# Cross-attention in a decoder layer: the mask's fetch one unit ahead, the row maxima on other steps

## The reference

```python
q = jnp.einsum('oc,bct->bot', Wq, target) + bq[None, :, None]
k = jnp.einsum('oc,bcs->bos', Wk, source) + bk[None, :, None]
v = jnp.einsum('oc,bcs->bos', Wv, source) + bv[None, :, None]
# q, k, v reshaped to (b, 16 heads, 16, 512)
dot = jnp.einsum('bhdt,bhds->bhts', q, k) / math.sqrt(HEAD_DIM)
mask = target_mask[:, :, :, None] * source_mask[:, :, None, :]
dot = mask * dot - (1.0 - mask) * NEG
amap = jax.nn.softmax(dot, axis=-1) * mask
out = jnp.einsum('bhts,bhds->bhdt', amap, v)
```

## Time and profile before

| | |
|---|---|
| median of 3 runs (lowest, highest) | 4616.4 us (4610.94, 4616.81) |
| the profiled execution's own time | 4613.8 us |
| its span, first to last instruction | 4612.0 us |
| mean granted TensorE clock | 0.959 |
| TensorE, VectorE, ScalarE busy | 91%, 70%, 48% of the span |

### The profile page before, as it was taken

One profiled execution on the slowest core, in us unless ns is written; L12 is line 12 of the kernel. 1 busy time (PEld: TensorE's weight loads), 2 busy tenths in 40 slices (PEclk: granted clock), 3 DMA queues, 4 the chain that ended last, 5 costly groups with the idle time before them and its releaser, 6 DMA issues. The chain is left out here.

```text
span 4612.0 us, 78540 instructions
## 1 busy us (share of the span) xinstructions
PE 4198.6 (91%) x27808; PEld 3133.2 (68%) x27808; DVE 3208.1 (70%) x6426; ACT 2230.6 (48%) x4057; POOL 623.2 (14%) x571
## 2 busy tenths in 40 slices
PE   3999999999999999999999999995788888489998
PEld 2777777777777777777777777773344444168887
DVE  3788888888888888888888888884555555532222
ACT  2555655555555655555555555552344444311111
POOL 1010010000110001100011000102133323411110
PEclk8999999999999999999999999996889989789999
DMA  2000000000000000000000000002545453000001
GB/s 70 1 15 15 11 15 11 16 10 11 15 15 11 10 11 15 15 11 11 11 16 15 11 13 9 15 1 51 82 81 86 81 85 64 38 23 19 19 14 37
DMA packets 66482, 122.17 MB, mean 26 GB/s; under 512 B 10476, under 2 KB 12396, under 8 KB 65548
## 3 DMA queue, kind: packets, MB, share of 16 engines
q1 hardware_dynamic: 63628, 115.69, 11.7%
q10 hardware_dynamic: 2432, 1.05, 0.1%
HBM read 93.05 MB, written 21.50 MB: 25 GB/s over the span
## 5 line engine op out<-in xcount | busy, mean ns | idle before, releaser
L387 PE MATMUL pj<-xh,w_hi 128*128 128x512 f32 x1536 | 688.2, 448 | 31.4 <-ACT conv_k L618 17.0
L387 PE MATMUL pj<-xh,w_lo 128*128 128x512 f32 x1536 | 607.7, 396 | 0.0
L387 PE MATMUL pj<-xl,w_hi 128*128 128x512 f32 x1536 | 602.7, 392 | 0.0
L1503 DVE TENSOR_REDUCE row_max<-s 128x1 f32<-128x512 f32 x512 | 341.8, 685 | 261.0 <-PE s L1257 256.9
L1437 ACT ACTIVATE probs<-s 128x512 f32<-128x512 f32 x512 | 290.3, 595 | 332.7 <-PE s L1281 265.8
L998 POOL CAST w_hi<-w_raw 128x512 fp32r<-128x512 f32 x96 | 73.8, 769 | 2083.8 <-PE pj L387 2079.7
L387 PEld LDWEIGHTS pj<-xh,w_hi 128*128 128x128 f32 x1536 | 291.1, 189 | 80.7 <-issue 32.3
L387 PEld LDWEIGHTS pj<-xh,w_lo 128*128 128x128 f32 x1536 | 289.2, 188 | 67.2
L689 ACT ACTIVATE kk_masked<-tp 128x512 f16<-128x512 f32 x320 | 191.4, 598 | 291.2 <-PE tp L493 288.1
L387 PEld LDWEIGHTS pj<-xl,w_hi 128*128 128x128 f32 x1536 | 292.7, 191 | 49.9 <-issue 14.8
L1281 PE MATMUL s<-q_stack,k_stack 128*128 128x512 f32 x512 | 247.0, 484 | 66.8 <-ACT probs L1437 52.0
(11 more groups left out here) (272 smaller groups left out, 10477.6 us busy)
## 6 DMA issues: line engine op xcount, KB each, us to landing
w_raw<-in_w_in SPq DMA_DIRECT2D x128, 256.0 KB, 2.6
q_stack<-qk_parts SPq DMA_DIRECT2D x128, 128.0 KB
k_stack<-qk_parts SPq DMA_DIRECT2D x128, 128.0 KB
f_raw<-in_f_w SPq DMA_DIRECT2D x32, 256.0 KB, 2.6
x_all<-in_x SPq DMA_DIRECT2D x4, 1024.0 KB, 9.2
source<-in_ctx SPq DMA_DIRECT2D x8, 512.0 KB
qk_parts<-q_hi SPq DMA_DIRECT2D x16, 256.0 KB, 2.4
qk_parts<-q_lo SPq DMA_DIRECT2D x16, 256.0 KB, 2.0
```

What stands on the lines that cost most here:

```text
L387: mm = pe.matmul(pj[j % 2][:, :], a[:, j, k * P:(k + 1) * P], b[:, k, bp * WIN:(bp + 1) * WIN], start=(n == 0), stop=(n == 3 * KT - 1))
L1503: dve.reduce_max(mx[g % 2][:, i:i + 1], s1[n % 2][:, :], AX_X).then_inc(E["rm"].sem, 1)
```

## The change

It touches `cross_attention` alone and leaves every operation in place; it moves them.

- The mask's DMA to 128 partitions leaves `load` and becomes `load_mask`. It is issued at the end of the odd unit before the batch is wanted (and for the first two batches in the start), after a wait for the last keys that use the old mask.
- LEAD goes from 28 to 30.
- Maxima of groups 0, 1, 2: turned at steps 11, 19, 27 (from 13, 21, 29), the rest at 12, 20, 28, sent at 13, 21, 29, fetched as before at 20, 28 and 4. Group 3: turned at 3, rest at 4, sent at 5, fetched at 12.
- `act_out` of the unit before at step 3 instead of 4, its denominators turned at 5 to 8 instead of 8 to 11, their reciprocal at 9 instead of 12.

```diff
--- before.py
+++ after.py
@@ -1058,7 +1058,7 @@
 QD = HH // 2
 UNITS = 2 * BATCH
 NEG = 1e6
-LEAD = 28
+LEAD = 30
 STEPS, SETS = 4 * HH, HH
 R_MASK, R_MAX, K_ROWS = 4 * XD, P - 2, P
 
@@ -1154,8 +1154,12 @@
                     E["pv"].wait(sp, b * 2 - 1, 0)
                     E["full"].wait(sp, b * 2 - 1, 1)
                 sp.dma_start(src[:, :, :], a["ctx"][b]).then_inc(E["src"].sem, 32)
+                sp.dma_start(mr4[:, :], a["mask"][b].to_broadcast([4, HID])).then_inc(E["mr4"].sem, 16)
+
+            def load_mask(b):
+                if b:
+                    E["full"].wait(sp, b * 2 - 1, 1)
                 sp.dma_start(mbp[:, :], a["mask"][b].to_broadcast([P, HID])).then_inc(E["mb"].sem, 16)
-                sp.dma_start(mr4[:, :], a["mask"][b].to_broadcast([4, HID])).then_inc(E["mr4"].sem, 16)
 
             def parts(u, f, side):
 
@@ -1189,6 +1193,7 @@
                         .then_inc(done.sem, 16)
 
             def start():
+                load_mask(0)
                 load(0, True)
                 for side in range(2):
                     parts(0, 0, side)
@@ -1199,6 +1204,7 @@
                     parts(1, 1, side)
                 stack(1, 1, 0, None)
                 stack_masks(0, 1, 0)
+                load_mask(1)
 
             start()
             for u in range(UNITS):
@@ -1213,6 +1219,8 @@
                     parts(u + 2, f, 1)
                     stack(u + 2, f, 0, u)
                     stack_masks(b + 1, f, 0)
+                    if f and b + 2 < BATCH:
+                        load_mask(b + 2)
 
 
         def pe_queries(pe, u, b, f):
@@ -1348,20 +1356,20 @@
                     pe_queries(pe, u + 2, b + 1, f)
                 if n == 12 and has2:
                     pe_keys(pe, u + 2, b + 1, f)
-                if 8 <= n < 12 and not is_first(u):
-                    if n == 8:
+                if n == 3:
+                    pe_turn_max(pe, u, 3)
+                elif n in (11, 19, 27) and has1:
+                    pe_turn_max(pe, u + 1, n // 8 - 1)
+                if 5 <= n < 9 and not is_first(u):
+                    if n == 5:
                         E["mxl"].wait(pe, u, 3)
-                    pe_denominators(pe, u - 1, n - 8)
+                    pe_denominators(pe, u - 1, n - 5)
                 if 18 <= n < 22 and not is_first(u):
                     if n == 18 and has2:
                         E["full"].wait(pe, u + 2, 1)
                     elif n == 18 and has1:
                         E["vsb"].wait(pe, u + 1, 0)
                     pe_spread(pe, u - 1, n - 18)
-                if n == 5:
-                    pe_turn_max(pe, u, 3)
-                elif n in (13, 21, 29) and has1:
-                    pe_turn_max(pe, u + 1, n // 8 - 1)
             if not has1:
                 pe_values(pe, u, f, SETS - 1)
                 for t in range(4):
@@ -1425,7 +1433,7 @@
 
         def act_unit(act, u, b, f, has1, has2):
             for n in range(STEPS):
-                if n == 4 and not is_first(u):
+                if n == 3 and not is_first(u):
                     act_out(act, u - 1, 1)
                 if n == 20:
                     act_out(act, u, 0)
@@ -1439,15 +1447,15 @@
                     act_part(act, u + 2, n // 14)
                 if n == 4:
                     act_max_in(act, u, f, 2)
+                elif n == 3:
+                    act_max(act, u, 3)
                 elif n == 5:
-                    act_max(act, u, 3)
-                elif n == 7:
                     act_max_out(act, u, 3)
                 elif n == 12:
                     act_max_in(act, u, f, 3)
+                elif n in (11, 19, 27) and has1:
+                    act_max(act, u + 1, n // 8 - 1)
                 elif n in (13, 21, 29) and has1:
-                    act_max(act, u + 1, n // 8 - 1)
-                elif n in (15, 23, 31) and has1:
                     act_max_out(act, u + 1, n // 8 - 1)
                 elif n in (20, 28) and has1:
                     act_max_in(act, u + 1, 1 - f, n // 8 - 2)
@@ -1536,15 +1544,15 @@
                     dve_maximum(dve, u, ahead)
                 elif has1:
                     dve_maximum(dve, u + 1, ahead - STEPS)
-                if n == 6:
+                if n == 4:
                     dve_max_rest(dve, u, 3)
-                elif n in (14, 22, 30) and has1:
+                elif n in (12, 20, 28) and has1:
                     dve_max_rest(dve, u + 1, n // 8 - 1)
                 if n == 2 and has1:
                     dve_source_values(dve, u + 1, 1 - f)
                 if n == 4 and has2 and f == 0:
                     dve_target(dve, b + 1, False)
-                if n == 12 and not is_first(u):
+                if n == 9 and not is_first(u):
                     dve_recip(dve, u - 1)
                 if n == 24 and not is_first(u):
                     dve_out(dve, u - 1)
```

## The result

| | before | changed |
|---|---|---|
| median of four runs of each (us) | 4613.67 (4609.63 to 4616.81) | 4570.73 (4565.36 to 4571.19) |
| ratio | | 0.9905, 95% interval 0.9888 to 0.9922 |
| profiled execution, its span (us) | 4613.8, 4612.0 | 4571.15, 4569.4 |

The change takes 43 us off. It is faster, and by more than this kernel's measurement can miss, but by little more than half of the forecast 76. 4571 lies inside the range (4512 to 4576), outside the forecast's own 4525 to 4558, and beside the time of rival 1, 4573.

The account below looks back on a forecast made before the run. TensorE was taken as nearly the bound in cross-attention, slowed by stops rooted in two DMA waits (maxima, mask). Terms -40 - 39 - 10 + 3 + 11 - 1 = -76 gave 4541 us; range 4512 to 4576.

Parts of the forecast that it names:

- rival 1: Maxima still wait, at step 27 and step 0 instead of 28; only the mask's -40 remains, about 4573 us; chance 0.17.
- The mask one unit ahead: Even units: VectorE's mask_quarter no longer waits for the mask's DMA; 6.67 us in six units, -40 us.
- The maxima two steps earlier: Every unit: ScalarE's exponential at step 28 no longer waits for the sent maxima to land in DRAM; -39 us.
- step 27: ScalarE's act_max there may wait for the earlier group's maxima to land; 0.2 us taken, over 14 units +3.
- What comes in its place: Next unit's first score waits for the maxima fetched at step 28: 0.3 us, or 1.5 in six odd units; +11.
- Nothing at steps 3 to 5: No stop from group 3's act_max and rest there; a stop at these steps would make the forecast fail.
- The half clock: TensorE's half clock at the unit's start goes with the step-28 stop; 0.8 us thirteen times, -10 us.
- even units of 41 us or less: Sign of being right: even units last at most 41 us and lie within 2 us of odd ones.
- a clock of 1.00 through most units: Sign of being right: TensorE's granted clock stays full through most cross-attention units.
- Rival 2: Nothing takes the old waits' place and the clock comes back wholly; -106, 4510 us; chance 0.20.
- Rivals 3: No effect: something equally late stands behind the mask and behind the maxima; 4616 us; chance 0.04.
- rival 4: Slower: group 3's act_max at step 3 waits for group 2's landing; about 4635 us at 15 us landing; chance 0.02.

Follow-up runs that it names:

- experiment 1: The kernel before with only the mask's load moved to the end of the odd unit, maxima and denominators on their old steps; 4585.7 us, ratio 0.9935.
- Experiment 3: The changed kernel with SyncE waiting for a unit's first score before issuing the next unit's odd heads' stacks; 4529.9 us, ratio 0.9815.
- Experiments 4: The changed kernel with work left out: from unit 2 on, the stack transfers move about half their bytes, in the same number of transfers; 4499.8 us, ratio 0.9751.
- experiment 10: The changed kernel with the even heads' query stacks issued first and from step 15 on, mask and odd heads' stacks unchanged; 4497.8 us, ratio 0.9753.
- Experiment 11: The changed kernel with the even heads' stacks ordered four of queries, then four of keys, none issued earlier; 4528.0 us, ratio 0.9821.
- experiment 6: Experiment 3's kernel with the mask's load moved right behind the even unit's first score, ahead of the odd heads' stacks; 4518.8 us, ratio 0.9792.
- experiments 4 and 7: The second of the pair: experiment 6's kernel with the even heads' query stacks issued first and from step 15 on; 4491.0 us, ratio 0.9727.

## Why the prediction was right, and where its size was off

**The mask one unit ahead: the wait went, the price was too high.** VectorE makes the target and the quarter one behind the other, where it stood 4.22 us between them (its timeline in even unit 8, steps 4 and 5):

```profile
3604.58 0.98 DVE L1482 TENSOR_SCALAR target<-x_all,x_mv,x_rstd 128x512 f32 x2
3605.49 0.41 DVE L1486 TENSOR_SCALAR mask_quarter<-mask_prep 128x512 f32<-128x512 f32 x1
```

The even units' longer pace is gone. But -40 was priced as if the bytes vanished with the wait; experiment 1 measured -28. The 262 KB lengthen the maxima's landing in the odd unit (63.1 us for 54.7, and 10.8 us for the seven odd units) and, with both parts in, the fetch's.

**The maxima two steps earlier: right.** The step-28 stop is gone, and step 27 waits 0.37 us in unit 7 (the forecast took 0.2, the other bound was 2.1). The drain explained this landing: it took 6.1 us and not the 7.8 of the earlier trace rows. TensorE's idle time before its scores and first-pass products was 46.1 us for ScalarE and 39.5 for VectorE in the thirteen units; now it is 2.9 and 0.2. So some 82 us of stops went, where the two terms hold about 64 (39 and six times 4.22).

**What comes in its place: this is the step that failed.** The forecast has +11, at 0.3 and 1.5 us a unit; measured are 55.5 us, at 2.2 to 2.7 and 5.3 to 6.0. Even its upper bounds, 1.2 and 3.2, make only 29. The sum counted what SyncE had issued ahead of the fetch. Two things were missing. First, the last score releases the odd heads' ten transfers behind the fetch. They did that before, too, 1.9 us behind it (the fetch at 3610.26):

```profile
3612.15 0.31 SPq L1179 DMA_DIRECT2D q_stack<-qk_parts  x1
```

But there the wait for the maxima had let the engines drain, and the fetch had landed after at most 2.64 us. Now they come 2.4 us behind it (3586.43 and 3588.80), while the engines are still full. Experiment 3 takes them away and gains 41 us, 30 of them in the loop. Second, the full engines cost a small transfer more than the drain of what was ahead: without the odd heads' stacks 1.4 to 2.1 and about 3.0 us of waiting are left. Experiments 4 and 10 take bytes away, or move them sooner, and the stop is gone. By what mechanism the small transfer is held up stays open.

**Nothing at steps 3 to 5:** right. The list has no such wait; the 4.7 us of act_max, in 11 pieces, stand late in a unit, in unit 7 at step 27.

**The half clock: forecast -25 in all, measured -9.** Besides the term's own 10, about 15 of the mask's 40 were clock (40 less six times 4.22). The new stops, 2.2 us and longer, all but the one ahead of unit 14, halve the clock just as the old ones did, for 3.4 and 6.8 us. All in all:

| us | forecast | measured |
|---|---|---|
| stops removed | -64 | -82.5 |
| stops that come instead | +14 | +52.8 in the thirteen units |
| other idle time | 0 | +2.6 |
| clock | -25 | -9.2 |
| start and end | -1 | -6.3 |
| sum | -76 | -42.6 of the span |

That the time fell inside the range is in part luck: 18 us more of stops went than forecast, against 39 more that came, and the range reached past rival 1. Two of the prediction's own signs of being right did not show: even units of 41 us or less (41.7), and a clock of 1.00 through most units (0.92 to 0.96).

**The rivals.** Rival 1 had the time (4573), and of its mechanism one half: step 0 gives back what step 28 had, step 27 does not; that the mask's part alone is left is not so either (28 and 37.5 alone). Rival 2's time comes with SyncE's transfers in another order: experiment 10 is below its 4510. Rivals 3 and 4 are excluded by the waits that went and by the steps 3 to 5 without one. (At 15 us, rival 4's own numbers give 4638 to 4641 us and not 4635; nothing hangs on it.)

The rule of the Trainium skill that each DMA engine takes the queues in turn (DMA: Bandwidth & Descriptors, Queues, rings and completion order) would have the fetch overtake the stacks. The 4.8 and 8.2 us against at most 2.64 with drained engines speak against it, as the earlier trace rows did. That page's rule on the semaphore's increment behind all earlier writes of an engine agrees with them; it does not by itself cover the stacks issued after the fetch, which experiment 3 shows to count. Which arbitration does that was not shown.

**What stays open.** Why the same eight transfers move faster as four query and four key stacks than in turn. Experiment 11 shows that they do, not why; no run separates the DRAM side from the partitions that they write.

## What to carry to other kernels

In this kernel a small transfer on which an engine waits had to be priced at more than the drain of the bulk transfers around it, those included that the waiting engine's own last work releases after it. Moving the consumer's steps shifts the wait to the next such transfer, and moving a load out of one stage puts its bytes in front of another. So put the bulk in order first: here the early query stacks alone were worth 48 us on the kernel before and 73 on the changed one, while with the queue in order the moved steps were worth 13.

## What the runs showed of the hardware

- The same transfers in another order ran at 129 to 142 GB/s instead of 114 to 129 with the engines about as busy, and the new order was worth 43 us of 4571 (experiment 11).
- A transfer of the maxima to q_stack took at most 2.6 us on drained DMA engines and 4.8 and 8.2 us beside stacks of 131 KB. Transfers issued 1.9 to 2.7 us after it counted where the engines were still full (experiment 3), and not where they had drained (before, and experiment 10).
- The clock went to 0.50 after stops of TensorE of 2.7 and 5.6 us, for 3.4 and 6.8 us. It did not fall after every such stop: ahead of unit 14 of the changed kernel TensorE stood 2.69 us and kept 1.00, and in experiment 6, with stops of 1.4 to 2.1 us, five of units 2 to 13 had a time at 0.50 and seven had none. Where no stop was above 1.0 us (experiments 4 and 7) it stayed at 1.00 over 480 us and more.
